# Alternating the score matmuls of the next unit with the transposed scores of the present one in the attention phase of a transformer block

## The chip, the core and the metric

The kernel runs on one core of a Trainium2 chip. The metric is the time on the device in microseconds (us), the median of several executions. A core has TensorE (PE, matmuls; it loads the stationary operand of each in a step of its own, PEld), VectorE (DVE), ScalarE (ACT), GpSimd (POOL) and SyncE (SP), each with its own queue of instructions taken in order; they wait for each other by semaphores. Matmuls write PSUM, which has 8 banks of 128 partitions by 512 numbers of 32 bits. TensorE's clock has two levels, 2.4 and 1.2 GHz; the profile shows the granted clock as 1.00 and 0.50. I call a stretch at 1.00 warm and one at 0.50 cold.

## The reference

Input x is 32 sequences of 256 tokens with 128 features. The function is a block of three layers: half a mixture of experts, causal attention, half a mixture of experts.

```python
x = x + 0.5 * ffn(layernorm(x))          # 8 experts, 2 per token, and a shared one
x = x + attn(layernorm(x))
x = x + 0.5 * ffn(layernorm(x))

def attn(x):                             # 16 heads of 8 features, sequence 256
    Q, K, V = x @ W_Q.T, x @ W_K.T, x @ W_V.T        # split into heads
    s = einsum('bhqd,bhkd->bhqk', Q, K) / sqrt(8)
    s = where(causal, s, -inf)
    p = softmax(s, axis=-1)
    return einsum('bhqk,bhkd->bhqd', p, V).reshape(...) @ W_O.T
```

## The kernel before

The three layers run one after the other. The change is in the second, `attention_phase`. It works on chunks of two sequences (512 tokens), 16 in all; one turn of the loop does one chunk and prepares the next. `run_pairs` peels the first two and the last two chunks and runs the rest as a loop with two turns in its body.

A turn has 8 **units**, for the two sequences b and, in each, four j. A unit is four heads. Their queries and keys (three copies of 8 features and a row for the maximum: split into a high and a low half in 16 bits) lie in the 32 partitions `unit_rows(j)` of `q_pack` and `k_pack`, so each of these matmuls uses 32 rows of the array, a different 32 for each j. I number the units of a turn 0 to 7 (4b + j).

The softmax needs each row's maximum before the exponential, so the scores are computed twice. In a unit PE issues:

- **T** (`scores_t`, L953): the transposed scores of this unit, keys by queries, 8 matmuls: two of 256 columns into `prob_bank[0]` (T0), two of 256 into `prob_bank[1]` (T1), four of 128 into `prob_bank[2]` (T2). ACT takes the exponential of each bank (L1144), POOL masks (L1186).
- **C and S** (`scores`): the scores of a unit five ahead (`unit_ahead`; its j is always (j + 1) mod 4), queries by keys, in three parts. Each part takes one of the two banks `score_bank` in turn: first a matmul of the full array that writes the causal term (L926: C0 with 512 columns, C1 and C2 with 256), then the heads added to it (L931: S0 is 4 matmuls of 128 columns, S1 and S2 are 2 of 256). DVE takes the row maxima of the part (L1066); the next part but one waits for that (`wait_count(pe, max_done, n - 1)`), since it has the same bank.
- **W** (`weigh`, L970): the probabilities of the unit before times V, in four groups of 32 array columns.
- **jobs** from the table `PLACES`, in three places of each unit: the projections (q, k, v), their packing (Q.., K..), the maxima put into the packed queries (m..), outputs (o.., y., z.) and the transposed input (x). They use two banks in turn; a job waits until the one before the last has been taken by ACT or DVE (`begin`).

PE's order in a unit was: T, jobs of place 0, C0 S0 C1 S1, jobs of place 1, W, C2 S2, jobs of place 2. DVE's order: jobs of place 0, maxima of parts 0 and 1, jobs of place 1, maximum of part 2, jobs of place 2. Each engine has this order in its own `turn` function; nothing is scheduled at run time.

Of the kernel before, what the change touches and what calls it, by code (L numbers as in the profile page):

```python
# [12 lines left out]
P = 128  # L13
SEQ = 256
# [9 lines left out]
GROUPS = 4  # L24
# [721 lines left out]
def attention_phase(nc, x, consts, w, norms):  # L746

    with ExitStack() as ctx:
# [20 lines left out]
        q_pack = [sb(f"q_pack{s}", [P, GROUPS, CHUNK], F16) for s in range(2)]  # L769
        k_pack = [sb(f"k_pack{s}", [P, GROUPS, CHUNK], F16) for s in range(2)]  # L770
# [9 lines left out]
        score_bank = [bank(f"score{s}") for s in range(2)]  # L780
# [6 lines left out]
        buffers_set = sem("buffers_set")  # L787
# [30 lines left out]
        def unit_rows(j):  # L818
            return slice(ROWS * j, ROWS * (j + 1))

        def turn_jobs(do, c, slot, names):

            for name in names:
                if has_job(name, c - SHIFT[name]):
                    do(c - SHIFT[name], (slot - SHIFT[name]) % 2, name)

        @block.tensor
        def _(pe):
# [78 lines left out]
                                                start=True, stop=True)  # L907
                last.then_inc(done, 1)

            def scores(c, slot, b, j, parts=(0, 1, 2)):  # L910

                if j == 0 and parts[0] == 0:

                    wait_taken(pe, c, f"Q{b}1")
                    wait_taken(pe, c, f"K{b}1")
                rows, first = unit_rows(j), b * SEQ
                for i in parts:
                    n = c * 24 + b * 12 + 3 * j + i

                    wait_count(pe, max_done, n - 1)  # L920
                    dst = score_bank[(3 * j + i) % 2]
                    groups = range(GROUPS) if i == 0 else range(2 * i - 2, 2 * i)
                    keys = P if i == 0 else SEQ
                    view = dst[:, :].rearrange("p (h k) -> p h k", k=keys)

                    nc.tensor.matmul(view[:, :, keys - P:keys], consts["ident_b"][:, :],  # L926
                                     consts["causal"][:, :].unsqueeze(1).to_broadcast([P, len(groups), P]),
                                     start=True, stop=False, skip_group_check=True)
                    q0 = first + (0 if i == 0 else P)
                    for h, g in enumerate(groups):  # L930
                        last = nc.tensor.matmul(view[:, h, :], q_pack[slot][rows, g, q0:q0 + P],  # L931
                                                k_pack[slot][rows, g, first:first + keys], start=False,
                                                stop=(h == len(groups) - 1), skip_group_check=True)
                    last.then_inc(scored, 1)

            def scores_t(c, slot, b, j):

                rows, first = unit_rows(j), b * SEQ
                unit = c * 2 * UNITS + b * UNITS + j
                if j == 0:  # L940

                    wait_taken(pe, c, f"m{b}0")
                    wait_taken(pe, c, f"m{b}1")
                for i in range(3):

                    wait_count(pe, exp_done, unit * 3 - 2 + i)

                    pe.wait_ge(buffers_set, 1)
                    keys = slice(first, first + P) if i < 2 else slice(first + P, first + SEQ)
                    queries = slice(keys.start, first + SEQ)  # L950
                    width = queries.stop - queries.start
                    for h, g in enumerate(range(2 * i, 2 * i + 2) if i < 2 else range(GROUPS)):
                        last = nc.tensor.matmul(prob_bank[i][:, h * width:(h + 1) * width],  # L953
                                                k_pack[slot][rows, g, keys], q_pack[slot][rows, g, queries],
                                                start=True, stop=True)
                    last.then_inc(st_done, 1)

            def weigh(c, slot, b, j):

# [15 lines left out]
            def turn(c, slot):  # L975
                for b in range(2):
                    for j in range(UNITS):
                        scores_t(c, slot, b, j)
                        places = PLACES[b * UNITS + j]
                        turn_jobs(job, c, slot, places[0])  # L980
                        ahead = unit_ahead(c, slot, b, j)
                        if ahead:
                            scores(*ahead, parts=(0, 1))
                        turn_jobs(job, c, slot, places[1])
                        if j > 0:
                            weigh(c, slot, b, j - 1)
# [18 lines left out]
        def _(dve):  # L1005
# [52 lines left out]
            def maxima(c, b, j, parts=(0, 1, 2)):  # L1058

                for i in parts:  # L1060
                    n = c * 24 + b * 12 + 3 * j + i

                    dve.wait_ge(scored, n + 1)
                    src = score_bank[(3 * j + i) % 2][:, :].rearrange("p (h k) -> p h k", k=P if i == 0 else SEQ)
                    dst = (neg_max[b][:, 0, :, j, MAX_ROW] if i == 0 else neg_max[b][:, 1, 2 * i - 2:2 * i, j, MAX_ROW])
                    nc.vector.tensor_reduce(dst, src, AX.X, ALU.max, negate=True).then_inc(max_done, 1)  # L1066

            def turn(c, slot):
                for b in range(2):
                    for j in range(UNITS):  # L1070
                        places = PLACES[b * UNITS + j]
                        turn_jobs(job, c, slot, places[0])
                        ahead = unit_ahead(c, slot, b, j)
                        if ahead:
                            maxima(ahead[0], *ahead[2:], parts=(0, 1))
                        turn_jobs(job, c, slot, places[1])
                        if ahead:
                            maxima(ahead[0], *ahead[2:], parts=(2,))
                        if b == 1 and j == 1:
                            norm(c + 2)  # L1080
                        if b == 1 and j == 2:
                            scale(c + 2)
                        turn_jobs(job, c, slot, places[2])
# [187 lines left out]
```

## Time and profile before

| | |
|---|---|
| three executions | 1431.63, 1465.17, 1488.01 us; median 1465.17 |
| the profiled execution, first to last instruction | 1465.3 us; the page gives no other time for it |
| PE busy | 1384.4 us, 94% |
| DVE, ACT, POOL busy | 77%, 59%, 38% |
| mean granted clock of TensorE | 0.931 |
| attention phase | from about 405 to 1082 us |

The page puts PE first by far. The mean granted clock is below 1 because TensorE was cold in a few stretches. The table of stages shows them in the attention phase (us from the start of the span): until about 493, 599 to 609, 681 to 688, 760 to 766, 838 to 845, and 917 to 985. The five that begin at 599 or later all begin right after the loop jumps back.

### The profile page before, as it was taken

The numbers are of one execution on the slowest core, as the hardware profiler recorded it, in microseconds if no ns is written. First come the engines' busy times: TensorE is split into PE (matmuls) and PEld (weight loads), VectorE is DVE, ScalarE is ACT, GpSimd is POOL, SyncE is SP. The second block draws the span as 40 slices with busy tenths as digits, with TensorE's granted clock in tenths as the row PEclk, the third lists the DMA queues.
The fourth block names the chain that finished last, engine by engine and source line by source line (L and its number), as shares of the span: only waits on it lengthen the run. The fifth ranks groups of instructions, "written<-read, shape, count | busy, mean of one in ns | idle before, by whom it ended". The sixth has DMA issues, their size and how long they took to land. (4 is left out here: it accounts for less than half of the span.)

```text
span 1465.3 us, 32010 instructions
## 1 busy us (share of the span) xinstructions
PE 1384.4 (94%) x9476; PEld 643.6 (44%) x9476; DVE 1121.2 (77%) x2686; ACT 857.6 (59%) x1509; POOL 553.2 (38%) x658
## 2 busy tenths in 40 slices
PE   5999999999889999998989899999989999999998
PEld 2343433334334555454545455445543434343343
DVE  7888889888754677676767677457768888888976
ACT  5666666666433566565656565346665666666564
POOL 3455445545402123222323222113334545544544
PEclk9999999999955799899999999559999999999999
DMA  6000000000000000000000000000000000000000
GB/s 171 1 1 0 0 0 0 0 0 0 1 0 1 1 2 2 2 1 2 2 2 1 2 2 2 1 1 2 2 1 8 8 14 14 8 14 7 14 7 22
DMA packets 21412, 11.86 MB, mean 8 GB/s; under 512 B 960, under 2 KB 21312, under 8 KB 21312
## 3 DMA queue, kind: packets, MB, share of 16 engines
q1 hardware_dynamic: 21312, 10.43, 2.5%
q8 instruction: 75, 1.23, 0.4%
q14 instruction: 25, 0.20, 0.0%
HBM read 6.23 MB, written 4.19 MB: 7 GB/s over the span
## 5 line engine op out<-in xcount | busy, mean ns | idle before, releaser
L666 POOL TENSOR_TENSOR h_lo<-h,h_hi 128x512 f16<-128x512 f32 x288 | 337.2, 1171 | 388.1 <-ACT h_hi L619 364.0
L1066 DVE TENSOR_REDUCE neg_max_at<-score_at 128x2 f16<-128x512 f32 (+1 forms) x384 | 257.3, 694 | 127.8 <-PE score_at L931 125.8
L1186 POOL TENSOR_SCALAR_AFFINE_SELECT probs_at<-probs_at 128x512 f32<-128x512 f32 x256 | 156.3, 634 | 448.3 <-ACT probs_at L1144 448.1
L619 ACT ACTIVATE h_hi<-h 128x512 f16<-128x512 f32 x288 | 180.5, 627 | 127.0 <-DVE h L419 125.2
L1144 ACT ACTIVATE probs_at<-prob_at 128x512 f32<-128x512 f32 x384 | 201.2, 600 | 52.2 <-PE prob_at L953 51.9
L419 DVE TENSOR_TENSOR h<-prod,gate_b 128x512 f32<-128x512 f32 x256 | 174.9, 683 | 53.5 <-PE gate_b L523 53.2
L413 DVE TENSOR_TENSOR prod<-silu,b 128x512 f32<-128x512 f32 x256 | 175.5, 686 | 38.4 <-ACT silu L608 24.1
L608 ACT ACTIVATE silu<-a 128x512 f32<-128x512 f32 x288 | 170.7, 593 | 57.3 <-PE a L510 50.1
L931 PE MATMUL score_at<-k_pack_at,q_pack_at 32*128 32x128 f16 (+1 forms) x1024 | 165.7, 266 | 0.0
L926 PE MATMUL score_at<-causal,ident_b 128*128 128x256 bf16 (+1 forms) x384 | 132.7, 346 | 5.5 <-DVE neg_max_at L1066 5.2
L953 PE MATMUL prob_at<-q_pack_at,k_pack_at 32*128 32x256 f16 (+1 forms) x1024 | 117.3, 259 | 13.8 <-issue 13.8
L970 PE MATMUL o_at<-probs_at,v_ones_at 128*32 128x256 f32 (+1 forms) x2048 | 123.4, 364 | 1.2 <-POOL probs_at L1186 1.0
L1150 ACT ACTIVATE o_t_at<-o_at 128x256 f32<-128x256 f32 x128 | 49.1, 383 | 111.8 <-PE o_at L970 110.1
L510 PE MATMUL b<-xt_hi,w_hi 128*128 128x512 f16 x288 | 112.8, 392 | 0.0
L540 PE MATMUL y_b<-h_hi,w_hi 128*128 128x512 f16 x288 | 109.3, 379 | 2.7 <-POOL h_lo L666 2.7
L510 PE MATMUL a<-xt_hi,w_hi 128*128 128x512 f16 x288 | 110.5, 384 | 0.0
L510 PE MATMUL a<-xt_hi,w_lo 128*128 128x512 f16 x288 | 110.2, 383 | 0.0
L510 PE MATMUL a<-xt_lo,w_hi 128*128 128x512 f16 x288 | 110.2, 382 | 0.0
L510 PE MATMUL b<-xt_hi,w_lo 128*128 128x512 f16 x288 | 110.0, 382 | 0.0
L510 PE MATMUL b<-xt_lo,w_hi 128*128 128x512 f16 x288 | 110.0, 382 | 0.0
L540 PE MATMUL y_b<-h_lo,w_hi 128*128 128x512 f16 x288 | 109.3, 379 | 0.0
L540 PE MATMUL y_b<-h_hi,w_lo 128*128 128x512 f16 x288 | 109.3, 379 | 0.0
(141 smaller groups left out, 2112.9 us busy)
## 6 DMA issues: line engine op xcount, KB each, us to landing
x<-in_L_attn_x_dram SPq DMA_DIRECT2D x16, 256.0 KB, 3.0
out_dram<-x SPq DMA_DIRECT2D x16, 256.0 KB, 2.3
raw_w<-in_L_ffn_w_dram SPq DMA_DIRECT2D x3, 512.0 KB, 4.9
raw_w<-in_L_ffn_sw_dram SPq DMA_DIRECT2D x3, 64.0 KB, 3.7
raw_attn<-in_L_attn_W_Q_dram SPq DMA_DIRECT2D x1, 64.0 KB, 4.9
raw_attn<-in_L_attn_W_K_dram SPq DMA_DIRECT2D x1, 64.0 KB, 3.6
raw_attn<-in_L_attn_W_V_dram SPq DMA_DIRECT2D x1, 64.0 KB, 3.3
raw_attn<-in_L_attn_W_O_dram SPq DMA_DIRECT2D x1, 64.0 KB, 3.4
```

Source lines behind the costliest of these rows:

```text
L413: nc.vector.tensor_tensor(prod[:, :], silu[k][:, :], b_bank[k][:, :], ALU.mult).then_inc(prod_done, 1)
L419: nc.vector.tensor_tensor(h[e % 3][:, :], prod[:, :], gate_bank[:, :], ALU.mult).then_inc(h_done, 1)
L510: last = nc.tensor.matmul(dst[k][:, :], ws[:, e, :], xs[slot][:, :], start=(i == 0), stop=(i == 2))
L540: last = nc.tensor.matmul(y_bank[:, :], ws[:, e, :], hs[k][:, :], start=(e == 0 and i == 0), stop=(e == STEPS - 1 and i == 2))
L608: nc.scalar.activation(silu[k][:, :], a_bank[k][:, :], ACT.Silu).then_inc(silu_done, 1)
L619: nc.scalar.activation(h_hi[k][:, :], h[k][:, :], ACT.Copy).then_inc(hhi_done, 1)
L666: nc.gpsimd.tensor_tensor(h_lo[k][:, :], h[k][:, :], h_hi[k][:, :], ALU.subtract).then_inc(hlo_done, 1)
L926: nc.tensor.matmul(view[:, :, keys - P:keys], consts["ident_b"][:, :], consts["causal"][:, :].unsqueeze(1).to_broadcast([P, len(groups), P ...
L931: last = nc.tensor.matmul(view[:, h, :], q_pack[slot][rows, g, q0:q0 + P], k_pack[slot][rows, g, first:first + keys], start=False, stop=(h ...
L1066: nc.vector.tensor_reduce(dst, src, AX.X, ALU.max, negate=True).then_inc(max_done, 1)
L1144: nc.scalar.activation(probs[j % 2][:, i, :], prob_bank[i][:, :], ACT.Exp, scale=SCALE).then_inc(exp_done, 1)
L1186: nc.gpsimd.affine_select(out=p, in_=p, compare_op=ALU.is_ge, fill=0.0, base=0, pattern=[[0, GROUPS], [1, P]], channel_multiplier=-1).then ...
```

## The change

PE's part of a unit is reordered by the new function `both`. It issues the causal terms C0 and C1 of the later unit first, both before any T. Then one T matmul is followed by as many score matmuls as have the same number of columns together: T0 S0 S0, T0 S0 S0, T1 S1, T1 S1. Then come T2, the jobs of places 0 and 1 together, W, C2 S2, and the jobs of place 2. T and S that stand side by side are in different rows of the array (`later_j != j`) and different banks. On DVE the maxima of parts 0 and 1 move ahead of the jobs of place 0. The last three units of the phase have no later unit and keep their order. The numbers of instructions do not change, nor what ACT, POOL and SP do.

The new function, from the diff, and the new order of a unit on PE and on DVE (the helpers `begin_scores`, `score_head`, `begin_t` and `head_t` hold the lines that `scores` and `scores_t` had, waits included):

```diff
@@ PE @@
+            def begin_scores(c, b, j, i):
...
+                wait_count(pe, max_done, n - 1)
+                dst = score_bank[(3 * j + i) % 2]
...
+                nc.tensor.matmul(view[:, :, keys - P:keys], consts["ident_b"][:, :],
+                                 consts["causal"][:, :].unsqueeze(1).to_broadcast([P, len(groups), P]),
+                                 start=True, stop=False, skip_group_check=True)
+                return view, groups, keys
...
+            def begin_t(c, b, j, i):
...
+                wait_count(pe, exp_done, unit * 3 - 2 + i)
...
+            def both(c, slot, b, j, ahead):
+
+
+                later, later_slot, later_b, later_j = ahead
+                assert later_j != j
+                parts = [begin_scores(later, later_b, later_j, i) for i in range(2)]
+                for i in range(2):
+                    begin_t(c, b, j, i)
+                    beside = len(parts[i][1]) // 2
+                    for h in range(2):
+                        head_t(slot, b, j, i, h)
+                        for k in range(beside * h, beside * (h + 1)):
+                            score_head(later_slot, later_b, later_j, i, parts[i], k)
+                scores_t(c, slot, b, j, parts=(2,))
...
             def turn(c, slot):
                 for b in range(2):
                     for j in range(UNITS):
-                        scores_t(c, slot, b, j)
                         places = PLACES[b * UNITS + j]
-                        turn_jobs(job, c, slot, places[0])
                         ahead = unit_ahead(c, slot, b, j)
                         if ahead:
-                            scores(*ahead, parts=(0, 1))
+                            both(c, slot, b, j, ahead)
+                        else:
+                            scores_t(c, slot, b, j)
+                        turn_jobs(job, c, slot, places[0])
                         turn_jobs(job, c, slot, places[1])
...
@@ DVE @@
                         places = PLACES[b * UNITS + j]
-                        turn_jobs(job, c, slot, places[0])
                         ahead = unit_ahead(c, slot, b, j)
                         if ahead:
                             maxima(ahead[0], *ahead[2:], parts=(0, 1))
+                        turn_jobs(job, c, slot, places[0])
                         turn_jobs(job, c, slot, places[1])
```

PE in unit 3 of the first turn, before. `prob_at` rows are T, `score_at` rows C (from `causal`) and S, `job_at<-ident,neg_max_at` the jobs m10 and m11, `o_at` W; the last row is the T of unit 4.

```order
L953 MATMUL prob_at<-q_pack_at,k_pack_at 128x128 x3
L905 MATMUL job_at<-ident,neg_max_at 128x128 [waits job_taken0_at,max_done_at]
L905 MATMUL job_at<-ident,neg_max_at 128x128 x3
L905 MATMUL job_at<-ident,neg_max_at 128x128 [waits job_taken1_at,max_done_at]
L905 MATMUL job_at<-ident,neg_max_at 128x128 x3
L926 MATMUL score_at<-causal,ident_b 128x512 [waits max_done_at,job_taken1_at,job_taken0_at]
L931 MATMUL score_at<-k_pack_at,q_pack_at 128x128 x4
L926 MATMUL score_at<-causal,ident_b 128x2x128 [waits max_done_at]
L931 MATMUL score_at<-k_pack_at,q_pack_at 128x256 x2
```

The same place now, from the last T of unit 3 to the first T of unit 4.

```order
L966 MATMUL prob_at<-q_pack_at,k_pack_at 128x128 x3
L905 MATMUL job_at<-ident,neg_max_at 128x128 [waits job_taken0_at,max_done_at]
L905 MATMUL job_at<-ident,neg_max_at 128x128 x3
L905 MATMUL job_at<-ident,neg_max_at 128x128 [waits job_taken1_at,max_done_at]
L905 MATMUL job_at<-ident,neg_max_at 128x128 x3
L1006 MATMUL o_at<-probs_at,v_ones_at 32x256 [waits o_done_at,masked_at]
L1006 MATMUL o_at<-probs_at,v_ones_at 32x256 x3
L1006 MATMUL o_at<-probs_at,v_ones_at 32x128 x4
L924 MATMUL score_at<-causal,ident_b 128x2x128 [waits max_done_at]
L934 MATMUL score_at<-k_pack_at,q_pack_at 128x256 x2
L924 MATMUL score_at<-causal,ident_b 128x512 [waits max_done_at]
L924 MATMUL score_at<-causal,ident_b 128x2x128 [waits max_done_at]
```

Four rows of scores stood between the m jobs and what follows them, and are gone from there (in later turns the job y1 stands right behind the m jobs). And the second causal term, which waits for the maximum of the part just before it in its bank, now follows that part's matmuls with one causal term between.

PE in unit 1 of the first turn, now: the alternating stretch.

```order
L924 MATMUL score_at<-causal,ident_b 128x512 [waits max_done_at]
L924 MATMUL score_at<-causal,ident_b 128x2x128 [waits max_done_at]
L966 MATMUL prob_at<-q_pack_at,k_pack_at 128x256 [waits buffers_set_at,exp_done_at]
L934 MATMUL score_at<-k_pack_at,q_pack_at 128x128 x2
L966 MATMUL prob_at<-q_pack_at,k_pack_at 128x256
L934 MATMUL score_at<-k_pack_at,q_pack_at 128x128 x2
L966 MATMUL prob_at<-q_pack_at,k_pack_at 128x256 [waits buffers_set_at,exp_done_at]
L934 MATMUL score_at<-k_pack_at,q_pack_at 128x256
L966 MATMUL prob_at<-q_pack_at,k_pack_at 128x256
L934 MATMUL score_at<-k_pack_at,q_pack_at 128x256
L966 MATMUL prob_at<-q_pack_at,k_pack_at 128x128 [waits buffers_set_at,exp_done_at]
```

Before, these were six T rows in a run, then C0 and its four heads, then C1 and its two. Now the array changes between matmuls of 128 and of 32 rows once in this stretch, not four times.

DVE in unit 3 of the first turn, before and now: the two jobs m10 and m11 (`q_pack_at<-job_at,q_pack_at`) and the maxima.

```order
L1038 TENSOR_TENSOR q_pack_at<-job_at,q_pack_at 128x4x128 [waits job_written0_at]
L1038 TENSOR_TENSOR q_pack_at<-job_at,q_pack_at 128x4x128 [waits job_written1_at]
L1066 TENSOR_REDUCE neg_max_at<-score_at 128x4 [waits scored_at]
L1066 TENSOR_REDUCE neg_max_at<-score_at 128x2 [waits scored_at] x2
```

```order
L1103 TENSOR_REDUCE neg_max_at<-score_at 128x4 [waits scored_at]
L1103 TENSOR_REDUCE neg_max_at<-score_at 128x2 [waits scored_at]
L1075 TENSOR_TENSOR q_pack_at<-job_at,q_pack_at 128x4x128 [waits job_written0_at]
L1075 TENSOR_TENSOR q_pack_at<-job_at,q_pack_at 128x4x128 [waits job_written1_at]
L1103 TENSOR_REDUCE neg_max_at<-score_at 128x2 [waits scored_at]
```

The two maxima now stand ahead of the two jobs.

## Rows read from the trace of the kernel before

**Rows 1.** The page: granted clock in 40 slices of 36.6 us.

```profile
PEclk9999999999955799899999999559999999999999
```

**Rows 2.** Stages: from:to, us, busy PE PEld DVE ACT POOL, clock, DMA, GB/s.

```profile
430.30:488.00 57.70, 57.70 (x336) 26.45 (x334) 28.30 (x54) 22.59 (x44) 10.99 (x18) 0.50 0.00 1
701.67:737.53 35.86, 35.86 (x368) 19.91 (x366) 28.30 (x60) 23.15 (x47) 10.93 (x18) 1.00 0.01 1
1076.40:1080.40 4.00, 2.36 (x26) 1.55 (x26) 1.38 (x5) 0.59 (x2) 0.00 (x0) 1.00 0.00 0
```

**Rows 3.** PE in order of time, warm: start us, duration, line, operation [idle before].

```profile
719.94 0.83 PE L953 MATMUL prob_at<-q_pack_at,k_pack_at 32*128 32x256 f16 x8
720.70 0.39 PE L926 MATMUL score_at<-causal,ident_b 128*128 128x512 bf16 x1
721.02 0.39 PE L931 MATMUL score_at<-k_pack_at,q_pack_at 32*128 32x128 f16 x4
721.34 0.28 PE L926 MATMUL score_at<-causal,ident_b 128*128 128x256 bf16 x1
721.56 0.39 PE L931 MATMUL score_at<-k_pack_at,q_pack_at 32*128 32x256 f16 x2
721.88 0.39 PE L838 MATMUL job_at<-xt_hi,attn_hi 128*128 128x512 f16 x1
722.11 0.38 PE L838 MATMUL job_at<-xt_hi,attn_lo 128*128 128x512 f16 x1
...
722.63 0.86 PE L970 MATMUL o_at<-probs_at,v_ones_at 128*32 128x256 f32 x16
...
728.72 0.39 PE L931 MATMUL score_at<-k_pack_at,q_pack_at 32*128 32x256 f16 x2
729.04 0.39 PE L867 MATMUL job_at<-q_stack_at,sel_q 128*128 128x256 f16 x2
```

**Rows 4.** PE in order of time, cold, in the first turn.

```profile
430.29 1.48 PE L953 MATMUL prob_at<-q_pack_at,k_pack_at 32*128 32x256 f16 x8
431.70 0.61 PE L926 MATMUL score_at<-causal,ident_b 128*128 128x512 bf16 x1
432.24 0.60 PE L931 MATMUL score_at<-k_pack_at,q_pack_at 32*128 32x128 f16 x4
432.78 0.39 PE L926 MATMUL score_at<-causal,ident_b 128*128 128x256 bf16 x1
433.10 0.60 PE L931 MATMUL score_at<-k_pack_at,q_pack_at 32*128 32x256 f16 x2
```

**Rows 5.** ACT and DVE in order of time, warm, beside Rows 3.

```profile
720.44 1.57 ACT L1144 ACTIVATE probs_at<-prob_at 128x512 f32<-128x512 f32 x3 [0.96 <-PE prob_at L953]
722.74 1.21 ACT L1119 ACTIVATE q_stack_at<-job_at 64x512 f16<-64x512 f32 x2 [0.72 <-PE job_at L838]
723.43 1.39 DVE L1028 TENSOR_TENSOR q_stack_at<-job_at,q_stack_at 64x512 f16<-64x512 f32 x2 [0.69 <-ACT q_stack_at L1119]
729.18 0.69 DVE L1066 TENSOR_REDUCE neg_max_at<-score_at 128x2 f16<-128x512 f32 x1
```

**Rows 6.** DVE and PE in order of time: PE waits for a maximum, cold.

```profile
424.15 0.70 DVE L1066 TENSOR_REDUCE neg_max_at<-score_at 128x2 f16<-128x512 f32 x1 [0.16 <-PE score_at L931]
424.90 1.03 PE L905 MATMUL job_at<-ident,neg_max_at 128*128 128x128 f16 x8 [0.79 <-DVE neg_max_at L1066]
```

**Rows 7.** DVE and PE in order of time, last turn: m jobs, then y1.

```profile
1064.29 0.62 PE L905 MATMUL job_at<-ident,neg_max_at 128*128 128x128 f16 x8
1064.73 1.29 DVE L1038 TENSOR_TENSOR q_pack_at<-job_at,q_pack_at 128x512 f16<-128x512 f32 x2 [0.49 <-PE job_at L905]
1065.56 0.41 PE L890 MATMUL job_at<-ident,y_at 128*128 128x128 f32 x2 [0.65 <-DVE q_pack_at L1038]
```

**Rows 8.** PE in order of time: the first T after the loop's jump.

```profile
679.99 0.82 PE L953 MATMUL prob_at<-q_pack_at,k_pack_at 32*128 32x256 f16 x8 [2.97 <-issue]
```

**Rows 9.** Page, costliest groups, W: busy us, mean ns | idle before.

```profile
L970 PE MATMUL o_at<-probs_at,v_ones_at 128*32 128x256 f32 (+1 forms) x2048 | 123.4, 364 | 1.2 <-POOL probs_at L1186 1.0
```

More of the change, by code:

```diff
@@ L908, in job @@
                 last.then_inc(done, 1)
-            def scores(c, slot, b, j, parts=(0, 1, 2)):
-                if j == 0 and parts[0] == 0:
+            def begin_scores(c, b, j, i):
+                if j == 0 and i == 0:
                     wait_taken(pe, c, f"Q{b}1")
                     wait_taken(pe, c, f"K{b}1")
-                rows, first = unit_rows(j), b * SEQ
-                for i in parts:
[L918 to L934, printed above, removed]
@@ L936, in scores_t @@
-            def scores_t(c, slot, b, j):
-                rows, first = unit_rows(j), b * SEQ
+                n = c * 24 + b * 12 + 3 * j + i
+                wait_count(pe, max_done, n - 1)
+                dst = score_bank[(3 * j + i) % 2]
+                groups = range(GROUPS) if i == 0 else range(2 * i - 2, 2 * i)
+                keys = P if i == 0 else SEQ
+                view = dst[:, :].rearrange("p (h k) -> p h k", k=keys)
+                nc.tensor.matmul(view[:, :, keys - P:keys], consts["ident_b"][:, :],
+                                 consts["causal"][:, :].unsqueeze(1).to_broadcast([P, len(groups), P]),
+                                 start=True, stop=False, skip_group_check=True)
@@ new lines, in begin_scores, with score_head @@
+                return view, groups, keys
+            def score_head(slot, b, j, i, part, h):
+                view, groups, keys = part
+                rows, first = unit_rows(j), b * SEQ
+                q0 = first + (0 if i == 0 else P)
+                last = nc.tensor.matmul(view[:, h, :], q_pack[slot][rows, groups[h], q0:q0 + P],
+                                        k_pack[slot][rows, groups[h], first:first + keys], start=False,
+                                        stop=(h == len(groups) - 1), skip_group_check=True)
+                if h == len(groups) - 1:
+                    last.then_inc(scored, 1)
@@ L939, in scores_t, with scores @@
+            def scores(c, slot, b, j, parts=(0, 1, 2)):
+                for i in parts:
+                    part = begin_scores(c, b, j, i)
+                    for h in range(len(part[1])):
+                        score_head(slot, b, j, i, part, h)
+            def begin_t(c, b, j, i):
                 unit = c * 2 * UNITS + b * UNITS + j
-                if j == 0:
+                if j == 0 and i == 0:
                     wait_taken(pe, c, f"m{b}0")
                     wait_taken(pe, c, f"m{b}1")
[L944 to L955, printed above, removed]
-                    last.then_inc(st_done, 1)
@@ new lines, in begin_t, with head_t @@
+                wait_count(pe, exp_done, unit * 3 - 2 + i)
+                pe.wait_ge(buffers_set, 1)
+            def head_t(slot, b, j, i, h):
+                rows, first = unit_rows(j), b * SEQ
+                keys = slice(first, first + P) if i < 2 else slice(first + P, first + SEQ)
+                queries = slice(keys.start, first + SEQ)
+                width = queries.stop - queries.start
+                groups = range(2 * i, 2 * i + 2) if i < 2 else range(GROUPS)
+                last = nc.tensor.matmul(prob_bank[i][:, h * width:(h + 1) * width],
+                                        k_pack[slot][rows, groups[h], keys], q_pack[slot][rows, groups[h], queries],
+                                        start=True, stop=True)
+                if h == len(groups) - 1:
+                    last.then_inc(st_done, 1)
```

5 lines of the change are left out of this document (added).

## The prediction

> **What bounds the kernel now.** I read the page first, then stages, then the engines in order of time. The change touches only the attention phase, and there PE is the bound: in a warm turn of 35.86 us PE is busy for all 35.86, DVE for 28.30, ACT for 23.15; in a cold turn PE is busy for 57.70 of 57.70 [rows 2]. The reader is to see that no other engine is near and that the clock makes a factor of 1.6 on a turn. In order of time PE's starts follow each other without a gap [rows 3]. So what is taken from PE's chain counts in full, and so does each wait that PE has not had so far. The granted clock is low in slices 12 to 14 and in 26 and 27 [rows 1]; these hold two long cold stretches of the phase, some 63 and 68 us, and four short ones follow jumps of the loop, where PE stood for up to 2.97 us [rows 8].
>
> **What a unit gains.** I count from start to start. Warm, T takes 0.76 us, C0 0.32, S0 0.32, C1 0.22, S1 0.32: 1.94 us [rows 3]. A matmul of 512 columns of the full array behind another of its kind takes 0.23 (from 721.88 to 722.11), but C0, also 512 columns, 0.32 before heads of 32 rows [rows 3]. So a change between the two shapes costs about 0.10 us, and each of the five pieces has one in it. In the new order only two remain: C0 without one is 0.21, C1 with one 0.21, T2 (512 columns in all) with one 0.32. Where a job of place 2 stands before the unit (7 of 8), its own change goes too, 0.11; between units 3 and 4 there is no such job, and one change comes in that T behind S2 did not have.
>
> **The alternating stretch** is 1024 columns of T and 1024 of S. The trace does not show two different 32-row parts of the array at work together, so I bound it. Below: both run side by side, 1024 columns at 2.4 GHz, 0.43 us; the nearest row for it is W, which works in four column groups: its matmuls last 0.364 us on average, yet 16 of them are done in 0.86 [rows 3, 9]. Above: one after the other, 0.85. Between them lies a third bound, that each matmul needs a weight load of 128 columns. S0's four matmuls, each with its load, take 0.22 without the change of shape, 0.055 each [rows 3]; that is also what their columns need, so a load may be faster, but no row shows it faster. The stretch has 10, so 0.55 us. I take 0.55, as the nearest row is that of these very instructions.
>
> The Trainium skill, page "TensorE: Matmul & The Clock Gate", part 3 on packing small matmuls, says that matmuls in different row groups run together, a few nanoseconds apart. By that the stretch would be 0.43; the trace shows it for column groups alone.
>
> New sum of a unit: 0.21 + 0.21 + 0.55 + 0.32 = 1.29, against 1.94. With the 0.11 it saves 0.76, times 8, less 0.2 for unit 4: **5.9 us of a warm turn**.
>
> **What a unit loses: the wait of C1.** C1 needs the maximum of part 2 of the unit before. S2 starts at 728.72 and its maximum at 729.18 behind other DVE work, 0.46 later; with DVE free I take 0.42. The maximum takes 0.70 [rows 5], and PE goes on 0.05 after its end (424.85 to 424.90) [rows 6]: 1.17 us from S2's start to C1's. Before, T, a job, C0 and S0 stood between, over 1.4 us. Now only S2 (0.32), the job of place 2 and C0 (0.21) do. With a packing job (0.32 less the change, 0.22) PE waits 0.42: units 1, 2, 4 and 5, 1.7 in all. Unit 3 has no such job: 0.64. Unit 7 has z0 (0.34): 0.3. Unit 6 has v (0.66), but on DVE the low half of y0 stands ahead of the maximum and comes late from ACT, behind its three exponentials: 0.6. Unit 0 is the worst. Its job q passes ACT and DVE before the maximum: exponentials begin 0.50 after T and last 1.57, the copy to 16 bits begins, DVE follows 0.69 later and needs 1.42 for its two [rows 5]. T now starts at 0.42, so q's DVE work ends at 0.42 + 0.50 + 1.57 + 0.69 + 1.42 = 4.6, C1 may start at 5.35, and PE is there at 4.2: 1.1 us. Together 4.3 us a turn.
>
> **And the wait behind the m jobs.** y1 (unit 3) and x (unit 7) use the bank of the first m job, which DVE must have taken. In the last turn, where scores no longer stand between, y1 starts 1.27 us after the m jobs although DVE is free; 0.65 of it PE is idle [rows 7]. Before, C0 S0 C1 S1, 1.18 us, covered it. Now DVE also has the two maxima ahead, 0.60 each back to back: S0 is complete at about 0.95, the m job is taken at 0.95 + 1.20 + 0.70 = 2.85, y1 starts at 2.9; PE has finished both m jobs (0.49) at 1.3 + 0.5 = 1.8. With the wait of C1 in the unit, which moves both but not equally, 1.1 us for y1. For x the normalization (four pieces on DVE, before the maxima) adds some 0.3: 1.4. Together 2.5, and what stands behind y1 and x is W, C2 and S2, then the next C1.
>
> **Sum.** A warm turn: -5.9 + 4.3 + 2.5 = +0.9 us, 36.8 for 35.86. A cold turn: T 1.41, C0 0.54, S0 0.54, C1 0.32, S1 0.54, 3.35 together [rows 4]; new 0.43 + 0.32 + 1.10 + 0.54 = 2.39; saved with the change of shape (0.11) 1.07, times 8 less 0.2: 8.4. DVE is no slower when PE is, so the wait of C1 vanishes where a job stands (S2 0.54, job 0.43, C0 0.43, against 1.39 needed) and is 0.4 in unit 3; behind the m jobs I put 0.5 and 0.8. Net -6.7. Of the 15.4 turns with the change (three units have no later one) I take 2.6 as cold: 131 us of long stretches are 2.3 turns, and 0.3 for the short ones. 12.8 x 0.9 - 2.6 x 6.7 = 11.5 - 17.4 = -6. The profiled execution's span is 1465.3, the median 1465.17, so nothing is to be shifted: **1460 us**. The three executions lie 56 apart, much more than this sum.
>
> **Rivals.**
> B, the two row parts run fully side by side (0.43). Warm another -1.0 a turn, cold -1.9: 12.8 x -0.1 - 2.6 x 8.6 = -24, 1441. For it: W's column groups. Against: 0.055 a load. Chance 0.17.
> C, the change does not do what it says: T and S go one after the other. Then 2.4 more a warm turn, of which the waits give back 0.3, and cold 4.9 more: 12.8 x 3.0 - 2.6 x 1.8 = +34, 1499. Nothing in the trace excludes it. Chance 0.12.
> D, the new waits let the clock fall. At the end of the phase PE was busy 2.36 us of 4.00 at clock 1.00 [rows 2], and the clock fell right after; no gap there was over 1.1 us. In unit 3, y1's wait and that of C1, and in unit 7 that of x, make a stretch nearly as thin. I let a fall in unit 3 last until the q and k jobs of the next turn, the densest full-array work: half a turn at (51.0 - 36.8) / 2 = 7.1 us. It decides from 5 falls in the phase, past 1494; a fall every second turn gives 1510, in every turn 1551; I put 1530. Against it: the 2.97 us stops were needed for the others. Chance 0.20.
> The skill's same page, section on the second HAM failure mode, says that short idle times between groups of matmuls that cycle through PSUM banks make the clock go up and down. The fall at the phase's end agrees; by the rule D is the case.
> E, the clock comes back sooner, as the cold stretches are denser in work now or merely by luck: two long stretches of 2.2 turns at 14.2 less, 1429. For it: one of the three executions before took 1431.63. Chance 0.14.
> My own case has 0.37, with a range of its own from 1440 to 1485 (B's and half of C's stretch, and the waits a third more or less).
>
> **Numbers.** About 2% is what a measurement here can tell from no change: below 1436 or above 1494. Faster: E 0.12, B 0.05, own 0.02, 0.19. Slower: D 0.18, C 0.08, own 0.01, 0.27. Within: 0.54. The range goes from E to D's middle, 1428 to 1525, and leaves out the rest of either.
>
> **What would show it.** The alternating stretch, first T to T2, at 0.43, 0.55 or 0.85 us warm; T and score matmuls with starts that do not wait for each other. PE idle before the 256-column causal term, released by DVE's maximum, some 0.4 us in most units and over 1 us in unit 0; PE idle before y1 and x, released by DVE's `q_pack`. A warm turn of 36 to 37.5 us with PE busy some 30. Clock 1.00 through the warm turns, else D. I am wrong if DVE is ready earlier than I reckon (a warm turn near 32) or if long cold stretches come or go.

## The result, and the profile after

The changed kernel takes 1483.68 us (median of 4 executions, 1476.46 to 1813.54), the kernel before 1449.54 us with a fourth execution added (1431.63 to 1488.01). The ratio is 1.034, 95% interval 1.026 to 1.041: **slower by 3.4%**. This ratio, like those below, compares only the executions near the quickest of each kernel: here 1476.46, 1482.42 and 1484.95 us (mean granted clock 0.92; it was 0.63 at 1813.54) with 1431.63 and 1433.91. The two medians differ by 2.4%.

The page after: busy times and the granted clock in 40 slices.

```profile
PE 1308.6 (89%) x9476; PEld 612.2 (42%) x9476; DVE 1114.1 (76%) x2686; ACT 857.0 (58%) x1509; POOL 554.3 (38%) x658
...
PEclk8999999999956888998989798889999999999999
```

PE's busy time fell from 1384.4 to 1308.6 us, and the time rose. Before, the clock was low in two blocks [rows 1]; now it is a little low nearly all through the attention phase. The stretches at 0.50 between the first T and the last add up to 163 us before and 180 now. PE in order of time, unit 1 of a turn, at clock 1.00, whose pieces answer to those in [rows 3]; the first row is C0, which follows job q of unit 0.

```profile
732.45 0.38 PE L924 MATMUL score_at<-causal,ident_b 128*128 128x512 bf16 x1
733.78 0.28 PE L924 MATMUL score_at<-causal,ident_b 128*128 128x256 bf16 x1 [0.95 <-DVE neg_max_at L1103]
733.99 0.28 PE L966 MATMUL prob_at<-q_pack_at,k_pack_at 32*128 32x256 f16 x1
734.00 0.28 PE L934 MATMUL score_at<-k_pack_at,q_pack_at 32*128 32x128 f16 x2
734.11 0.27 PE L966 MATMUL prob_at<-q_pack_at,k_pack_at 32*128 32x256 f16 x1
734.12 0.27 PE L934 MATMUL score_at<-k_pack_at,q_pack_at 32*128 32x128 f16 x2
734.24 0.26 PE L966 MATMUL prob_at<-q_pack_at,k_pack_at 32*128 32x256 f16 x1
734.24 0.28 PE L934 MATMUL score_at<-k_pack_at,q_pack_at 32*128 32x256 f16 x1
734.35 0.27 PE L966 MATMUL prob_at<-q_pack_at,k_pack_at 32*128 32x256 f16 x1
734.36 0.27 PE L934 MATMUL score_at<-k_pack_at,q_pack_at 32*128 32x256 f16 x1
734.46 0.38 PE L966 MATMUL prob_at<-q_pack_at,k_pack_at 32*128 32x128 f16 x4
734.77 1.15 PE L881 MATMUL job_at<-ident,o_t_at 128*128 128x128 f32 x8
```

A T and an S matmul start within 0.02 us of each other: the two parts of the array work side by side, and the stretch takes 0.47 us here (0.44 in another unit, 699.96 to 700.40). With T2 it is 0.75 to 0.78 before the next job. The wait of C1 stands above it. The whole list of PE's waits in one turn without a jump, and then its timeline from unit 3's C0 to y1:

```profile
PE score_at L924 <- DVE neg_max_at L1103: 2.1, 5, 0.9
PE job_at L850 <- DVE q_pack_at L1075: 1.2, 1, 1.2
PE score_at L924 <- ACT k_pack_at L1164: 1.1, 1, 1.1
PE job_at L890 <- DVE q_pack_at L1075: 1.0, 1, 1.0
```

```profile
742.56 0.50 PE L924 MATMUL score_at<-causal,ident_b 128*128 128x512 bf16 x2 [1.15 <-ACT k_pack_at L1164]
...
743.75 0.62 PE L905 MATMUL job_at<-ident,neg_max_at 128*128 128x128 f16 x8
...
745.40 0.63 PE L890 MATMUL job_at<-ident,y_at 128*128 128x128 f32 x2 [1.03 <-DVE q_pack_at L1075]
```

The third wait was not in my sum: C0 of unit 3 belongs to a unit with j = 0 and waits until ACT has taken K01, a job that PE issues right ahead of it. Before, T stood between.

Stages (from:to, us, busy PE PEld DVE ACT POOL, clock, DMA, GB/s), cut from one unit 7 to the next: first the stretch before, with a jump, then the same turn as above; of it the piece with unit 3's two waits and what follows, then the same for its unit 7; then the piece with unit 3's two waits in the stretch before; last, the only stretch in which the clock never fell. They answer to [rows 2].

```profile
678.00:721.40 43.40, 33.27 (x367) 18.18 (x366) 27.94 (x61) 23.26 (x47) 11.02 (x18) 0.92 0.01 2
721.40:763.30 41.90, 36.27 (x367) 19.52 (x366) 28.17 (x61) 23.03 (x46) 10.96 (x18) 0.84 0.01 2
...
742.00:745.50 3.50, 1.91 (x25) 1.29 (x26) 2.04 (x4) 1.81 (x4) 0.84 (x2) 1.00 0.00 0
745.50:755.70 10.20, 9.89 (x71) 4.33 (x73) 4.58 (x8) 3.36 (x7) 1.61 (x3) 0.50 0.01 2
721.40:725.00 3.60, 2.11 (x27) 1.52 (x27) 3.60 (x9) 2.16 (x4) 1.23 (x2) 1.00 0.00 0
725.00:728.40 3.40, 3.40 (x29) 1.56 (x27) 1.49 (x3) 0.98 (x2) 0.00 (x0) 0.50 0.02 5
703.60:707.10 3.50, 1.98 (x26) 1.37 (x26) 2.11 (x4) 1.83 (x4) 0.91 (x2) 1.00 0.02 5
1019.40:1056.10 36.70, 30.85 (x367) 17.66 (x366) 27.88 (x61) 23.04 (x47) 10.97 (x18) 1.00 0.01 1
```

So a turn costs in two steps. By the waits alone it is 36.7 us, 0.8 more than before. And right behind the waits of unit 3, where PE was busy 1.91 us of 3.50, the clock falls for 10.2 us; behind x's wait in unit 7 for 3.4: 41.9 us. Before, a turn without a jump was 35.9 us and had none.

The fall is frequent, not certain. In the turn behind the jump the same two waits of unit 3 stand (1.05 and 1.03 us, PE busy 1.98 us of 3.50), and the clock stayed at 1.00. Counted from unit 0, each of the loop's twelve turns in the trace has one fall behind such waits: seven in unit 3, five in unit 7, none both. The stretch from 678.00 has only the one behind the jump (from 687.5, for 6.8 us), which the kernel before had too.

### The profile page after: what moved, and what is told of

It reads as the page before. It is cut to its first block and busy times, and to the rows that moved or that the text cites. A ratio compares the mean times of both kernels' runs of the same rounds, so it can differ in the third digit from the quotient of the medians.

```text
span 1474.7 us, 32010 instructions
## 1 busy us (share of the span) xinstructions
PE 1308.6 (89%) x9476; PEld 612.2 (42%) x9476; DVE 1114.1 (76%) x2686; ACT 857.0 (58%) x1509; POOL 554.3 (38%) x658
## 5 line engine op out<-in xcount | busy, mean ns | idle before, releaser
L608 ACT ACTIVATE silu<-a 128x512 f32<-128x512 f32 x288 | 170.9, 593 | 57.7 <-PE a L510 50.8
L924 PE MATMUL score_at<-causal,ident_b 128*128 128x256 bf16 (+1 forms) x384 | 127.9, 350 | 55.8 <-DVE neg_max_at L1103 30.0
L934 PE MATMUL score_at<-k_pack_at,q_pack_at 32*128 32x128 f16 (+1 forms) x1024 | 145.4, 266 | 0.0
L1006 PE MATMUL o_at<-probs_at,v_ones_at 128*32 128x256 f32 (+1 forms) x2048 | 130.9, 381 | 1.2 <-POOL probs_at L1223 1.0
L523 PE MATMUL gate_b<-gate_t,select_gate 16*128 16x512 f16 x256 | 98.9, 386 | 0.5 <-DVE h L419 0.5
```

The source lines that it names most:

```text
L608: nc.scalar.activation(silu[k][:, :], a_bank[k][:, :], ACT.Silu).then_inc(silu_done, 1)
L934: last = nc.tensor.matmul(view[:, h, :], q_pack[slot][rows, groups[h], q0:q0 + P], k_pack[slot][rows, groups[h], first:first + keys], star ...
L1006: last = nc.tensor.matmul(o_bank[g * ROWS:(g + 1) * ROWS, t * P:SEQ], v_ones[slot][:, 2 * b + t, GROUPS * g + j, :], src, start=(t == 0), ...
```

## Experiments

All are compared with runs of the kernel before on the same chip, whose median was 1433 to 1447 us.

**e1b: one part of the change alone, on the old order of PE.**

```diff
@@ DVE, kernel before @@
-                        turn_jobs(job, c, slot, places[0])
                         ahead = unit_ahead(c, slot, b, j)
                         if ahead:
                             maxima(ahead[0], *ahead[2:], parts=(0, 1))
+                        turn_jobs(job, c, slot, places[0])
```

> The kernel before with one part of the change: on DVE the maxima of parts 0 and 1 go ahead of the jobs of place 0; PE keeps its old order, nothing alternates. y1 and x on PE must then wait for the m jobs behind two maxima: m to y1 was 1.80 us, becomes about 3.2, so about 1.4 us of PE idle in unit 3 and in unit 7. My theory (waits of PE bring the clock down): the waits cost 2 x 1.4 x 16 = 45 us and falls of the clock come in units 3 and 7 of many turns, so 1495 to 1560 us. Rival 1 (the alternating stretch brings the clock down): no new falls, about 1495. Rival 2 (the clock is chance, the waits are all): as rival 1.

Measured 1691.34 us, ratio 1.174 (1.168 to 1.180). In the profiled execution, which took 1724.49, the turns took 50 to 67 us. Two of them:

```profile
595.50:648.60 53.10, 50.21 (x367) 24.87 (x366) 29.46 (x64) 23.29 (x47) 10.94 (x18) 0.68 0.01 2
648.60:715.90 67.30, 62.65 (x367) 29.16 (x366) 29.31 (x61) 23.33 (x46) 10.94 (x18) 0.50 0.01 1
```

In the same trace y1 waits 1.44 us for DVE at 622.12, as expected, and the clock is low from 621.5 on for 112.6 us. PE had no other wait over 0.2 us in the 5 us ahead, so here a single wait of 1.44 us stands before a fall. The waits are worth some 45 us, the loss is 258: nothing alternates here, so rival 1 falls, and the waits alone do not make it. My range was too low, since I let a cold stretch end within the turn.

**e2b: T and S in `both` not alternating.**

```diff
                 for i in range(2):
                     begin_t(c, b, j, i)
-                    beside = len(parts[i][1]) // 2
                     for h in range(2):
                         head_t(slot, b, j, i, h)
-                        for k in range(beside * h, beside * (h + 1)):
-                            score_head(later_slot, later_b, later_j, i, parts[i], k)
+                for i in range(2):
+                    for k in range(len(parts[i][1])):
+                        score_head(later_slot, later_b, later_j, i, parts[i], k)
```

> The change, but with T0, T1, S0 and S1 one after the other in `both` instead of alternating; both causal terms still come first and all waits stay. The stretch should go from 0.44 us to 0.85, as two parts of the array no longer work together. My theory: 0.41 x 8 = 3.3 us more a warm turn, less a few tenths that the waits give back, and the falls of the clock stay: about 1520 to 1540. Rival 1 (the alternation brings the clock down): the falls in units 3 and 7 go, warm turns of about 38.5 and no cold time in most, 1480 to 1500. Rival 2: about 1530.

Measured 1492.49 us, ratio 1.042 (1.036 to 1.048). Missed: only some 9 us over the change, not 40. PE in one unit:

```profile
700.65 0.48 PE L966 MATMUL prob_at<-q_pack_at,k_pack_at 32*128 32x256 f16 x3
700.87 0.28 PE L934 MATMUL score_at<-k_pack_at,q_pack_at 32*128 32x128 f16 x2
700.97 0.27 PE L966 MATMUL prob_at<-q_pack_at,k_pack_at 32*128 32x256 f16 x1
701.00 0.27 PE L934 MATMUL score_at<-k_pack_at,q_pack_at 32*128 32x128 f16 x2
...
701.25 0.21 PE L966 MATMUL prob_at<-q_pack_at,k_pack_at 32*128 32x128 f16 x1
701.42 0.39 PE L867 MATMUL job_at<-k_stack_at,sel_k 128*128 128x256 f16 x2
```

From the first T to the next job it is 0.77 us, as in the change. S runs beside the last of T and beside T2. It is enough here that both kinds are near each other in the queue; that the fine alternation adds anything is not shown.

**e10: the same rows of the array.** The scores of parts 0 and 1 are those of other heads in this kernel.

```diff
-                            score_head(later_slot, later_b, later_j, i, parts[i], k)
+                            score_head(later_slot, later_b, j, i, parts[i], k)
```

> The change, but the score heads of `both` read the 32 rows of the present unit instead of those of the later one; so the scores of parts 0 and 1 are those of other heads. Nothing else moves. In the change, T, S and T2 take 0.75 us from the first T to the next job, as in e2b where they do not alternate. If that is the work of two parts of the array side by side, the same rows make it one after the other: 2560 columns, 1.07 us and a change of shape, 1.17. Then 0.42 x 8 = 3.4 us more a warm turn, more in the cold ones, less what the waits give back: 1515 to 1535. If the speed had another cause (loads hidden, fewer changes of shape), nothing changes: 1484.

Measured 1521.52 us (1500 to 1538), ratio 1.051 (1.040 to 1.062), the median inside the expected. T and S now start 0.11 us apart, each behind the one before:

```profile
699.96 0.27 PE L934 MATMUL score_at<-k_pack_at,q_pack_at 32*128 32x128 f16 x2
700.07 0.27 PE L966 MATMUL prob_at<-q_pack_at,k_pack_at 32*128 32x256 f16 x1
700.18 0.27 PE L934 MATMUL score_at<-k_pack_at,q_pack_at 32*128 32x256 f16 x1
```

The stretch from the first T to T2 takes 0.89 us (699.62 to 700.51), in place of 0.44 to 0.47. The only difference to the change is which 32 rows are used, so it is shown that different rows work side by side. What this is worth in time is less sure: 38 us by the medians, 25 by the ratios (1.051 and 1.034), whose intervals touch.

**e3b: the waits of y1 and x filled.**

```diff
+            def fill(n):
+
+                for _ in range(n):
+                    nc.tensor.matmul(o_bank[:, SEQ:2 * SEQ], consts["ident_b"][:, :],
+                                     consts["causal"][:, :].unsqueeze(1).to_broadcast([P, 2, P]),
+                                     start=True, stop=True, skip_group_check=True)
...
                         turn_jobs(job, c, slot, places[0])
+                        if ahead and j == 3:
+                            fill(8)
                         turn_jobs(job, c, slot, places[1])
```

> The change, with 8 matmuls of 256 columns of the full array between the m jobs and y1, and between the m jobs and x; they write an unused half of a bank and nobody reads them. They lie in PE's idle time of 1.03 and 1.21 us and need about 0.9, so they cost nothing in themselves. My theory: the clock falls after unit 7's wait go and those of unit 3 become rare (the wait of 1.05 us for K01 before it stays), cold time of 13 us a turn becomes 3 to 7, worth 2.5 to 5 us a turn: 1410 to 1450. Rival 1 (alternation) and rival 2 (waits alone, clock by chance): no change, about 1484.

Measured 1409.49 us, ratio 0.983 (0.979 to 0.987): 16 useless matmuls a turn make the changed kernel 74 us faster, and faster than the kernel before. A turn, and PE around y1 in unit 3:

```profile
691.60:728.90 37.30, 32.78 (x383) 19.14 (x382) 27.96 (x61) 23.05 (x46) 10.96 (x18) 1.00 0.00 0
```

```profile
711.61 0.50 PE L924 MATMUL score_at<-causal,ident_b 128*128 128x512 bf16 x2 [1.09 <-ACT k_pack_at L1173]
712.80 0.62 PE L905 MATMUL job_at<-ident,neg_max_at 128*128 128x128 f16 x8
713.26 1.04 PE L1014 MATMUL o_at<-causal,ident_b 128*128 128x256 bf16 x8
714.45 0.44 PE L890 MATMUL job_at<-ident,y_at 128*128 128x128 f32 x2 [0.16 <-DVE q_pack_at L1084]
```

The wait for K01 is still 1.09 us, and the clock stays at 1.00; in the whole loop it fell once, for 3.4 us. But something else went too. In the kernels before and after, PE stands behind the loop's jump (up to 2.97 us [rows 8]; after, up to 2.47 and a little later up to 2.05), and the clock falls there; in e3b it hardly stands, and the turns with a jump are as short as the others. So this run alone does not tell the two apart.

**e5: the same, but the added matmuls have 8 columns, and so fill nothing.**

```diff
-                    nc.tensor.matmul(o_bank[:, SEQ:2 * SEQ], consts["ident_b"][:, :],
-                                     consts["causal"][:, :].unsqueeze(1).to_broadcast([P, 2, P]),
+                    nc.tensor.matmul(o_bank[:, SEQ:SEQ + 8], consts["ident_b"][:, :], consts["causal"][:, 0:8],
```

> The change with the same 8 added matmuls in the same two places as in e3b, but of 8 columns each instead of 256, so that they fill next to nothing (some 0.2 us) of the waits of y1 and x. In e3b the loop's jump on PE also went from 3.3 us to 0.21, which was not expected, and took the falls after the jump away; this run has the same number of instructions. If e3b's gain came from the filled waits (my theory), the falls in units 3 and 7 come back and stay at 10 + 3 us a turn: with the jump short 1445 to 1460, with the jump long 1484. If it came from the instructions alone (the shorter jump, another place in memory), no falls in units 3 and 7 and about 1400 to 1410.

Measured 1460.87 us, ratio 1.017 (1.008 to 1.025). The jumps are short, and the clock falls again in unit 3 of every turn of the loop, for 10.2 us (twice 13.7), and not in unit 7:

```profile
716.00:756.60 40.60, 35.34 (x383) 19.60 (x382) 28.07 (x61) 23.05 (x47) 10.94 (x18) 0.87 0.00 0
```

So of the 74 us, about 51 (1460.9 to 1409.5) are what the filled waits give by the clock (a turn of 40.6 us becomes one of 37.3), and about 23 (1483.7 to 1460.9) go with the short jump. The two kernels ran on different chips; by the ratios, 1.017 and 0.983, it is about 48 and 25.

**e6: the kernel before with the thin matmuls.**

```diff
                             scores(*ahead, parts=(0, 1))
+                        if ahead and j == 3:
+                            fill(8)
                         turn_jobs(job, c, slot, places[1])
```

> The kernel before with the 8 thin matmuls (8 columns) behind the scores of units 3 and 7, ahead of y1 and x. They cost 16 x 0.2 to 0.3 us a turn pair at most, some 5 us in all. If the number of instructions in the loop decides the jump, it takes 0.2 us instead of 3.3 to 3.7 here too, and the five falls behind it (6.8 us cold or more each, turns of 43 instead of 36) go: 1433 - 5 x 6.5 + 5 = 1405. If the jump stays long: 1438.

Measured 1464.50 us (1430 to 1526), ratio 1.021 (1.001 to 1.040), with all four executions in it: missed. The profiled execution was the quickest. In it the turns behind the first, those with a jump as well, took 36.2 us, except around the first jump, where PE stood for 3.9 us and was cold for 47.8:

```profile
721.50:757.70 36.20, 36.20 (x383) 20.25 (x382) 28.28 (x61) 23.14 (x46) 10.94 (x18) 1.00 0.00 0
589.10:649.00 59.90, 55.97 (x384) 26.75 (x383) 29.60 (x61) 23.16 (x47) 10.94 (x18) 0.60 0.01 2
```

The jump's part came as expected, the time did not, and the executions spread over 96 us. I have a trace of one of the four alone; that the others had more such long stretches is a guess.

**e4b: C1 between the two alternating parts.**

```diff
-                parts = [begin_scores(later, later_b, later_j, i) for i in range(2)]
+                parts = [None, None]
                 for i in range(2):
+                    parts[i] = begin_scores(later, later_b, later_j, i)
                     begin_t(c, b, j, i)
```

> The change, but the second causal term stands between the parts (C0, T0 with S0 alternating, C1, T1 with S1 alternating, T2), no longer right behind C0. C1 then starts 0.3 us or more later than now against the maximum it needs: its waits (30 us in 81 places) mostly go, two changes of shape (0.2 us a unit) come. The waits of y1, x and that for K01 stay. My theory: 1.6 us more of matmuls and 2 to 2.5 us less of waits a turn, and the falls of the clock mostly stay as the long waits do: 1465 to 1490. Rival 1: falls stay. Rival 2: 1470.

Measured 1443.75 us, ratio 1.005 (1.001 to 1.009), better than expected. C1's waits between 440 and 1070 us of the span went from 28.3 us to 2.6. A turn without a fall is 35.1 us. In the loop there is no fall in unit 7 any more, but still one in unit 3 in six turns of twelve, mostly of 13.7 us:

```profile
469.30:504.40 35.10, 31.61 (x367) 17.72 (x366) 28.08 (x61) 23.39 (x47) 10.98 (x19) 1.00 0.01 1
698.80:739.50 40.70, 37.37 (x367) 20.04 (x366) 28.29 (x61) 23.48 (x46) 10.90 (x19) 0.83 0.01 2
```

**e7: the jobs of place 0 back ahead of the scores, on PE and DVE.** DVE's order is then that of the kernel before.

```diff
@@ PE; on DVE the same line moves ahead of maxima @@
                         ahead = unit_ahead(c, slot, b, j)
+                        turn_jobs(job, c, slot, places[0])
                         if ahead:
                             both(c, slot, b, j, ahead)
                         else:
                             scores_t(c, slot, b, j)
-                        turn_jobs(job, c, slot, places[0])
                         turn_jobs(job, c, slot, places[1])
```

> The change, but the jobs of place 0 stay ahead of the scores on PE and on DVE, as they were before: jobs 0, then C0 C1 and the alternating stretch, T2, jobs 1. The stretch (0.75 us and more with T2) and the causal terms then stand between the m jobs and y1 or x, and the m jobs cover K01. Waits left: m for the last maximum (1.17 us from S2's start, of which S2 gives 0.32: 0.85 in unit 3, 0.5 in unit 7), C1 as now in the other units, less where a job of place 0 stands. My theory: the waits of y1, x and K01, 3.3 us a turn, become 1.4, a warm turn is 34.5 instead of 36.7, and as no stretch has two long waits together the falls in units 3 and 7 become rare: 1400 to 1440. If the falls come from the alternating stretch, they stay and it is 1450 to 1470.

Measured 1403.63 us, ratio 0.977 (0.968 to 0.985). The waits of y1, x and of C0 for K01 are gone from the loop, the m jobs wait 12.9 us for maxima in 31 places (up to 0.8) and 4.6 us for K01 in 14. A turn is 34.6 us; alternating goes on as in the change, and the falls in units 3 and 7 are gone but for one:

```profile
688.10:722.70 34.60, 30.94 (x366) 17.52 (x366) 28.24 (x61) 22.61 (x47) 10.94 (x18) 1.00 0.01 2
```

**e8: e7 and e4b together.**

> e7 and e4b together: jobs of place 0 first, and C1 between the two alternating parts. The waits of C1 go as well. A warm turn of about 33 us (28.7 of matmuls, 1.7 more changes of shape, the waits of the m jobs, and unit 0's q): 1380 to 1410 if the falls behind the jump stay, as in e4b, 1360 to 1390 if they go.

Measured 1394.46 us, ratio 0.972 (0.960 to 0.983): a turn without and one with a jump.

```profile
751.40:784.90 33.50, 32.05 (x366) 17.71 (x366) 28.07 (x61) 23.21 (x46) 10.94 (x19) 1.00 0.01 2
784.90:824.50 39.60, 34.50 (x366) 18.43 (x366) 28.21 (x61) 23.49 (x46) 10.97 (x19) 0.91 0.01 2
```

**e9: e8 with a short jump.**

```diff
+            def fill(c, b, j, n):
+                wait_count(pe, max_done, c * 24 + b * 12 + 3 * j - 1)
+                for _ in range(n):
+                    nc.tensor.matmul(score_bank[(3 * j) % 2][:, 0:P], consts["ident_b"][:, :],
+                                     consts["causal"][:, :], start=True, stop=True, skip_group_check=True)
...
                         ahead = unit_ahead(c, slot, b, j)
+                        if ahead and j == 3:
+                            fill(ahead[0], *ahead[2:], 8)
                         turn_jobs(job, c, slot, places[0])
```

> e8 with 8 matmuls of 128 columns of the full array ahead of the m jobs (units 3 and 7), in the bank that C0 writes next. They need 0.44 us and lie in a wait of 0.85 and one of 0.5 us, so they cost nothing; e8 has hardly any falls in those units, so they gain little there. But with the added instructions I expect the short jump of e3b, e5 and e6 (0.21 us instead of 3.3 to 3.8): the turns of 39.6 to 40.2 us at the jumps become 33.5, 5 x 6.3 = 31 us less: 1394 - 31 = 1363. If the jump stays long, 1394.

Measured 1351.72 us (1345 to 1357), ratio 0.941 (0.937 to 0.945): **5.9% faster than the kernel before**. It writes the same output.

```profile
663.80:697.10 33.30, 32.75 (x385) 18.57 (x382) 27.97 (x61) 23.20 (x46) 10.87 (x19) 1.00 0.00 0
```

Every turn from 469 to 935 us is like this one (33.3 to 33.4 us), with or without a jump.

**e11: e1b with its waits filled.** 12 matmuls as in e3b, between S1 and y1 or x.

> e1b (the order of PE as before, maxima ahead of the jobs of place 0 on DVE) with 12 matmuls of 256 columns of the full array between the scores and y1, and between the scores and x: about 1.3 us in PE's waits of 1.5 us. They do no work that counts. My theory (idle PE brings the clock down): most of the 530 us of cold time in e1b's turns go, turns of 53 to 67 us become 39, so 15.4 x 3.1 = 48 us over before, and 5 short jumps give 30 back: 1445 to 1470 instead of 1691. If e1b was slow by the waits or the order themselves, it stays near 1691.

Measured 1488.32 us, ratio 1.034 (1.025 to 1.042), above the expected. It is 203 us less than e1b by added work. A turn is 38.9 us without a fall:

```profile
730.80:769.70 38.90, 38.84 (x391) 22.09 (x391) 28.25 (x61) 23.16 (x47) 10.94 (x18) 1.00 0.00 1
```

The expected jump was wrong: PE stands there for up to 4.3 us, longer than before, and all remaining falls of the loop are behind it. With 8 added matmuls in two places the jump was short in four kernels (in e6 but for the first), with 12 it is long. So it is not simply that more instructions help. What sets it stays open.

## Why the prediction was wrong

**The time lay in the range, the verdict did not.** I forecast no change (0.54), and it is slower by 3.4%. The failed step is the one that set the cold share of the phase: "Of the 15.4 turns with the change I take 2.6 as cold". It took the cold stretches of before as they were and counted a gain of 17.4 us on them, and the sum has no term for new falls; D, the waits bring the clock down, stood beside it as a rival at 0.20. D is what happened, once in every turn of the loop. Shown by: e3b against e5 (the same instructions, only wide enough to fill the waits: 51 us), e11 against e1b (203 us), and e7, where the waits are taken away by order.

That the time lies in the range, even in the 1440 to 1485 of my own case, is luck. The base of 1465 was 32 us above the executions of before that the ratio takes (1433), the 17.4 us of gain were not there, and the falls were missing. By an estimate from the traces it is 1433 + 12 for the waits (0.8 in each of 15.4 turns) + 43 for the falls (some 112 us of cold time behind the waits, at 5.2 us lost in 13.6) = 1488, against 1482, the median of the three executions of the change in the ratio.

**What D was worth.** I let a fall last half a turn, 7.1 us each, and reached 1551 for one in every turn (one in every second turn comes to 1505 at that price, not 1510). It lasts mostly 10.2 us in unit 3 and 3.4 in unit 7, and one of each makes the stretch of 41.9 us for 36.7: some 3 us a fall. So D's frequency was put too low and its price too high.

The Trainium skill's rule that I set beside it, short idle times between groups of matmuls that cycle through PSUM banks make the clock go up and down ("TensorE: Matmul & The Clock Gate", second failure mode), agrees with this trace: y1 and x wait for a bank, and the clock fell behind them, in unit 3 after PE had been busy 1.91 us of 3.50.

**The alternating stretch.** I took 0.55 us for the load of weights; it is 0.44 to 0.47, rival B's bound. The Trainium skill's rule on different row groups in the same page was right where I followed S0's four loads, whose 0.055 was the time of their columns and no bound at all. I had written that, and still took it.

**The waits.** The sum was 6.8 us a turn, counted from start to start. The profile lists 5.4 in the turn above, but it counts from the modelled end of the matmul before: C0's record lasts 0.38 us, while the next matmul could have started after 0.21. From start to start, in the stretch without a fall (from 1019.40), C1's waits are 3.8, against 4.3: behind job q 1.0 (1.1 forecast), behind v and y0 0.4 (0.6), and none in unit 3 (0.4). y1: 1.1 forecast, 1.3 measured. x: 1.4 and 1.4. Missing in the sum: 1.1 us for C0 of unit 3, which waits for K01 or, in this stretch, for Q01 beside it. The function's second line, a wait that comes only with j = 0, would have told. This wait stands in the same unit as y1's, and there the clock falls most often. Filling y1's wait was enough to stop that while K01's stayed (e3b); that taking K01's away would do it if y1's stayed is not shown.

**The warm turn.** 36.8 forecast, 36.7 measured, by two errors that cancel: the stretch is 0.9 us a turn shorter than I took it, and the waits are 7.5 in place of 6.8.

**The kernel before.** I set the sum against a median of three, 1465.17. With more executions it is 1433 to 1450. Its executions of 1432 to 1433 us have a mean granted clock of 0.956 to 0.961, the profiled one 0.931, which makes some 80 to 90 us less of cold time; so I take the second of its long cold stretches (60.6 us) and a part of the first for luck of an execution. This is an estimate: none of the 1432 us was traced, and e6's trace, of 1430 us, has two long stretches as well. My estimate of 6 us gained, against 1465, stood on cold turns that a usual execution has not. A turn of before without falls, 35.9, was the sounder base, and against it the same sum says slower by 0.9 us a turn.

**Rival C** (it runs one after the other) is excluded by e10. **Rival E** (long cold stretches come to an end sooner) looks true between the two traces, where the first turn took 45.2 us (from 432.0) in place of 57.7 and the second long stretch is absent. By the estimate above most of that is chance.

## What to carry to other kernels

Where the bound engine is TensorE at the high clock, price a new wait twice: its own length, and a fall of the clock behind it. Here that came behind waits of 1.1 and 1.0 us close together, and in e1b behind single ones of 1.44. Look for such waits, and try cheap matmuls in the gap as a probe; if time falls, order the work so that the gap goes. When work is moved earlier, list every wait that moves with it, those under conditions too, and what stood between it and its producer: here both causal terms first cost 3.2 us of waits a turn (C1 2.1, C0 for K01 1.1) and the small jobs behind the scores 2.2 (y1 and x), while C1 between the parts and the small jobs ahead (e8) kept the gain.

## What the runs showed that I had not expected

- Two kinds of matmuls in different 32 rows of the array overlap even when issued in runs of 4 (e2b): 0.77 us, against 0.75 when alternating.
- PE's stop behind the loop's jump, 2.0 to 4.3 us in the other kernels, was nearly absent in e3b, e5, e6 (but for its first jump) and e9, whose loop body holds 32 more matmuls. It is worth about 23 us by e5, the fall of the clock behind it included. e9 is 43 us quicker than e8, of which the jump is some 31 (five times 39.6 less 33.3); e8's trace also has a fall in unit 3 that e9's has not, and e9 fills a wait as well. The cause of the stop is open.
- A change of order on DVE alone (e1b) made the kernel 17% slower, of which its waits are 3%.
